# Adaptive-norm attention and feed-forward on one core: mixed adapter tiles moved into the down products, SyncE's queue re-ordered, style product issued a tile earlier, projections in the order Q, K, V

## What is computed

```python
W = weights[condition]                                # one 32x32 matrix per batch, of 16
h = einsum('bct,bcd->bdt', x, W)                      # "style" product
q, k, v = split(clip(einsum('bsd,ed->bse', h, w_qkv), -8, 8), 3)
q, k = layer_norm(q) * w + b, layer_norm(k) * w + b
p = softmax(q k^T * scale + alibi, causal)            # 32 heads of 16, 32 positions
x = x + einsum('bsd,ed->bse', p v, w_out)
y = einsum('bsi,boi->bso', x, weight[adapter_ids])    # one 512x512 adapter per batch, of 8
h = relu(y @ up_w) ** 2
shared = h @ down_w
routed = ((y @ fc1) @ expert) * sum(top2(y @ gate)) @ fc2
x = x + layer_norm(shared + routed) * gamma + beta
```

## Time and profile before

| | us |
|---|---|
| median of 3 runs | 1117.49 |
| lowest and highest | 1116.0, 1117.51 |
| the profiled execution, its own time | 1122.09 |
| its span in the trace | 1120.3 |
| TensorE busy within the span | 1063.7 (95%) |
| VectorE, ScalarE, GpSimd busy | 623.6, 572.7, 567.8 |

### The profile page before, as it was taken

One profiled execution on the slowest core, in us unless ns is written; L12 is line 12 of the kernel. 1 busy time (PEld: TensorE's weight loads), 2 busy tenths in 40 slices (PEclk: granted clock), 3 DMA queues, 4 the chain that ended last, 5 costly groups with the idle time before them and its releaser, 6 DMA issues.

```text
span 1120.3 us, 29460 instructions
## 1 busy us (share of the span) xinstructions
PE 1063.7 (95%) x12012; PEld 841.9 (75%) x12012; DVE 623.6 (56%) x1050; ACT 572.7 (51%) x955; POOL 567.8 (51%) x490
## 2 busy tenths in 40 slices
PE   5999999999999999999989995999999999999994
PEld 3878778888878887878777774675868777787883
DVE  4577767767675767676764333333544434454432
ACT  3576777777767778777774214224060514233220
POOL 5666877777776777776654222222242323233331
PEclk9999999999999999999999997999999999999997
DMA  6125454555545556556468835293616252130101
GB/s 254 62 79 174 170 185 168 178 189 173 192 149 178 177 190 202 182 169 171 153 242 305 316 102 152 67 215 105 168 64 202 65 192 64 64 85 29 47 29 37
DMA packets 99988, 166.59 MB, mean 149 GB/s; under 512 B 45648, under 2 KB 46416, under 8 KB 96016
## 3 DMA queue, kind: packets, MB, share of 16 engines
q1 hardware_dynamic: 90304, 140.97, 39.1%
q0 software_dynamic: 6064, 17.05, 5.2%
q10 hardware_dynamic: 3488, 6.70, 1.7%
HBM read 98.09 MB, written 40.89 MB: 124 GB/s over the span
## 4 chain that ended last, share of the span: by engine, by line
PE 82%; issue 4%; POOL 4%; DMA 3%; DVE 3%; ACT 2%; SPq 2%; ACTq 0%; POOLq 0%; DVEq 0%
PE banks L726 20%; PE pair L961 15%; PE banks L937 14%; PE banks L954 7%; PE banks L775 7%; PE banks L841 6%; PE pair L743 2%; PE banks L857 2%; PE pair L803 2%; POOL w_lo L1807 1%; PE banks L907 1%; PE banks L711 1%; DMA yT_lo<-y_part_low 1%; SPq L497 1%; POOL probs L1801 1%
## 5 line engine op out<-in xcount | busy, mean ns | idle before, releaser
L1807 POOL TENSOR_TENSOR w_lo<-w2t,w_hi 128x2048 fp32r<-128x2048 f32 x26 | 119.5, 4595 | 75.1 <-ACT w_hi L1129 75.1
L726 PE MATMUL banks<-wqkv_hi,h_hi 128*128 128x512 f32 x384 | 153.2, 399 | 3.2 <-DVE wqkv_lo L1604 0.5
L1872 POOL TENSOR_TENSOR u_lo<-act,u_hi 128x512 fp32r<-128x512 f32 x64 | 82.4, 1289 | 139.7 <-ACT u_hi L1342 139.7
L726 PE MATMUL banks<-wqkv_hi,h_lo 128*128 128x512 f32 x384 | 149.7, 390 | 0.0
L726 PE MATMUL banks<-wqkv_lo,h_hi 128*128 128x512 f32 x384 | 149.7, 390 | 0.0
L1896 POOL TENSOR_TENSOR frstd<-fve,cst 128x1 f32<-128x1 f32 x32 | 31.9, 997 | 186.4 <-DVE fve L1740 186.4
L1438 ACT ACTIVATE total<-banks,weight 128x512 f32<-128x512 f32 x32 | 22.0, 687 | 187.2 <-PE banks L954 187.2
L937 PE MATMUL banks<-yT_hi,up_hi 128*128 128x512 f32 x256 | 102.3, 400 | 11.9 <-ACT act L1338 11.9
L1733 DVE TENSOR_TENSOR total<-total,pair 128x512 f32<-128x512 f32 x32 | 22.0, 688 | 152.2 <-PE pair L961 152.2
L937 PE MATMUL banks<-yT_hi,up_lo 128*128 128x512 f32 x256 | 100.6, 393 | 0.0
L937 PE MATMUL banks<-yT_lo,up_hi 128*128 128x512 f32 x256 | 100.4, 392 | 0.0
(11 more groups left out here) (182 smaller groups left out, 2636.8 us busy)
## 6 DMA issues: line engine op xcount, KB each, us to landing
w2t<-in_w SPq DMA_DIRECT2D x26, 1024.0 KB
w<-in_w SPq DMA_DIRECT2D x24, 768.0 KB, 7.1
vx<-v_hl SPq DMA_DIRECT2D x128, 68.0 KB, 2.6
x1g<-x_rows SPq DMA_DIRECT2D x32, 256.0 KB, 2.8
kx<-k_hl SPq DMA_DIRECT2D x124, 64.0 KB
x_rows<-x1t SPq DMA_DIRECT2D x31, 256.0 KB, 2.3
y_rows<-ys SPq DMA_DIRECT2D x26, 256.0 KB, 3.3
w<-in_w SPq DMA_DIRECT2D x24, 256.0 KB, 2.8
```

Of the source, the lines that this page charges most:

```text
L726: m = e.matmul(into, a[:, c, :], b[:, n, c, :], start=(c == 0 and k == 0), stop=(c == KC - 1 and k == 2))
L1807: e.tensor_tensor(w2_lo[:, :, :], w2t[:, :, :], w2_hi[:, :, :].bitcast(F32), ALU.subtract).then_inc(d_wlo, 1)
L1872: e.tensor_tensor(u_lo[n % FC][:, :], act[n % 2][:, :], u_hi[n % FC][:, :].bitcast(F32), ALU.subtract) \
```

## The change

- late(m) is gone: the mixed tiles of all six groups are done among the down products (turn_mixed ahead of them; adapt_first after down(m, 0) and adapt_last after down(m, 1), in group 0 after down(0, 1) and down(0, 2)). Before, group 0 had them one tile later.
- SyncE's order is one for all: load_x1(4m+2), load_last(m); in group 0 then load_x1(3) and load_y(2) ahead of store_mixed(0); store_mixed(m), load_mixed(m+1), then load_x1(4m+3), load_y(m+2), and load_first(m+1) at the end.
- In attention, from tile 7 on, style is issued one iteration earlier and as its last product: style(i+2) after values(i-3) instead of style(i+1) after the projections. It now waits for add_x(i-4) of the same iteration (`upto(e, "x1", t - 6)` with t = i+2) and for slot_out of tile i-6. high_h and low_h of tile i+1 go to the start of the iteration on ScalarE and VectorE, GpSimd makes the style matrix one tile further ahead.
- The projections go in the order Q, K, V in all iterations; VectorE takes v after q and k. low_planes moves behind q's clip and statistics.
- In the drain, VectorE's last low_planes, low_o(T-4) and add_x(T-5), and ScalarE's high_o(T-4) come earlier.

```diff
--- before.py
+++ after.py
@@ -341,10 +341,6 @@
 
         return m < MIXED
 
-    def late(m):
-
-        return m < 2
-
     def upto(e, name, i):
 
         if i >= 0:
@@ -670,21 +666,22 @@
                     upto(e, "r", T - 1)
                     load_back(1, 0, 0, KC)
                     load_back(1, 1, 0, KC)
-                if late(m):
-                    load_x1(GROUP * m + 2)
+                load_x1(GROUP * m + 2)
                 if mixed_in(m):
                     load_last(m)
-                    if late(m):
-                        load_x1(GROUP * m + 3)
+                if m == 0:
+                    load_x1(3)
+                    load_y(2)
+                if mixed_in(m):
                     store_mixed(m)
-                    if mixed_in(m + 1):
-                        load_mixed(m + 1)
-                        load_first(m + 1)
-                if not late(m):
-                    load_x1(GROUP * m + 2)
+                if mixed_in(m + 1):
+                    load_mixed(m + 1)
+                if m:
                     load_x1(GROUP * m + 3)
-                if m + 2 < GROUPS:
+                if m and m + 2 < GROUPS:
                     load_y(m + 2)
+                if mixed_in(m + 1):
+                    load_first(m + 1)
 
             last_rows = [e.value_load(tile_rows[SEQ * b:SEQ * b + 1, TILES - 1:TILES], min_val=0, max_val=TOKENS - SEQ)
                          for b in range(BPT)]
@@ -702,7 +699,11 @@
                 upto(e, "x1", t - 6)
                 upto(e, "hlo", t - 1)
                 if style_tiled(t):
-                    upto(e, "cv", t - 1)
+                    upto(e, "cv", t - 2)
+                    if t == LAG + 1:
+                        upto(e, "klo", t - 3)
+                    else:
+                        e.wait_ge(d_mc, t - 1 - LAG)
                 for c in range(KC):
                     if style_tiled(t):
                         for k in range(2):
@@ -832,7 +833,7 @@
                     upto(e, "cq", s + LAG)
                     e.wait_ge(d_mc, s)
                 else:
-                    upto(e, "hlo", s + LAG + 1)
+                    upto(e, "cv", s + LAG)
                 pairs = [(xgT_hi, w2_lo, c) for c in range(KC)]
                 pairs += [(xgT_hi, w2_hi, c) for c in range(KC)] + [(xgT_lo, w2_hi, c) for c in range(KC)]
                 for k, (a, b, c) in enumerate(pairs):
@@ -928,7 +929,7 @@
                     e.wait_ge(m_up[1], 32)
                 if n >= 2:
                     e.wait_ge(S["relu"], n - 1)
-                if f == 1 and m and late(m - 1):
+                if f == 1 and m and mixed_in(m - 1):
                     e.wait_ge(d_mc, UNIFORM + m)
                 cols = slice(P * (f % KC), P * (f % KC) + P)
                 for c in range(KC):
@@ -947,8 +948,6 @@
                     e.wait_ge(m_down, 48)
                 if n >= 2:
                     e.wait_ge(S["tot"], n - 1)
-                if t == 1 and mixed_in(m) and not late(m):
-                    e.wait_ge(d_mc, UNIFORM + m + 1)
                 for c in range(KC):
                     for k, (a, b) in enumerate(((yT_hi, route_hi), (yT_hi, route_lo), (yT_lo, route_hi))):
                         i = e.matmul((B6, B7)[n % 2], a[m % 2][:, c, toks], b[:, c, :],
@@ -997,6 +996,8 @@
                 upto(e, "klo", i - 2)
                 if i > LAG:
                     e.wait_ge(d_mc, i - LAG)
+                if style_tiled(i + 1) and i + 1 < T:
+                    upto(e, "hlo", i + 1)
                 project(i, 2, B5, "pv")
 
             def turn_q(t):
@@ -1011,18 +1012,14 @@
             for i in range(T - 1):
                 if 0 < i < SHORT:
                     style(i + 1)
-                if i >= LAG:
-                    project_v(i)
                 project_q(i)
                 if i in (2, 3):
                     make_route(i - 1)
                 project_k(i)
                 if i == 0:
                     style(1)
-                if i < LAG:
-                    project_v(i)
+                project_v(i)
                 if i >= LAG:
-                    style(i + 1)
                     turn_slot(i - LAG, banks47)
                 if i >= 4:
                     turn_values(i - 4)
@@ -1041,6 +1038,8 @@
                     make_route(3)
                 if i >= 3:
                     values(i - 3)
+                if LAG - 1 <= i < T - 2:
+                    style(i + 2)
 
             project_q(T - 1)
             project_k(T - 1)
@@ -1085,18 +1084,9 @@
                     up(m, f)
                     if m == 0 and f == EARLY:
                         turn_gates(0)
-                    if mixed_in(m) and not late(m):
-                        if f == 3:
-                            e.wait_ge(S["route"], GROUP * m - 1)
-                            turn_mixed(m, B6)
-                        if f == 4:
-                            e.wait_ge(S["route"], GROUP * m)
-                            adapt_first(m, B7)
-                        if f == FC - 1:
-                            adapt_last(m, B7)
                 if ahead and m:
                     gate_products(m + 1)
-                if late(m):
+                if mixed_in(m):
                     e.wait_ge(S["relu"], FC * m + FC - 1)
                     turn_mixed(m, B2)
                 for t in range(GROUP):
@@ -1105,9 +1095,9 @@
                         gate_products(1)
                     if ahead and t == (0 if m else 2):
                         turn_gates(m + 1)
-                    if late(m) and t == (0 if m else 2):
+                    if mixed_in(m) and t == (0 if m else 1):
                         adapt_first(m, B3)
-                    if late(m) and t == (1 if m else 3):
+                    if mixed_in(m) and t == (1 if m else 2):
                         adapt_last(m, B3)
 
         @block.scalar
@@ -1293,7 +1283,7 @@
                                  scale=rstd[t % 2][:, n:n + 1]).then_inc(A[("qn", "kn")[n]], 1)
 
             for i in range(T - 1):
-                if i < SHORT:
+                if i < SHORT or i >= LAG:
                     high_h(i + 1)
                 if i == 0:
                     high_weights(3)
@@ -1314,7 +1304,6 @@
                 if i >= 1:
                     normalize(i - 1)
                 if i >= LAG:
-                    high_h(i + 1)
                     slot_in(i - LAG, banks47)
                 if i >= 4:
                     high_o(i - 4)
@@ -1366,9 +1355,9 @@
             scale_q(T - 2)
             high_q(T - 2)
             soft_exp(T - 3)
+            high_o(T - 4)
             scale_k(T - 1)
             high_k(T - 1, k_last)
-            high_o(T - 4)
             high_probs(T - 3)
             slot_out(LAST, B2)
             scale_q(T - 1)
@@ -1409,8 +1398,6 @@
                 ahead = m + 1 < GROUPS
                 for f in range(first_up(m), FC):
                     n = FC * m + f
-                    if mixed_in(m) and not late(m) and f == 4:
-                        mixed_turned(m, B6)
                     relu(n)
                     if ahead:
                         for c in turns(m, f):
@@ -1425,10 +1412,8 @@
                     high_u(n)
                 if ahead and m:
                     gates_out(m + 1)
-                if late(m):
+                if mixed_in(m):
                     mixed_turned(m, B2)
-                elif mixed_in(m):
-                    mixed_out(m, B7)
                 for t in range(GROUP):
                     n = GROUP * m + t
                     e.wait_ge(S["rp"], n + 1)
@@ -1639,24 +1624,22 @@
                 if i >= 4:
                     divide(i - 4)
                 if i >= LAG:
-                    take_v(i)
-                if i >= T - 8:
-                    low_planes(i - T + 8)
+                    low_h(i + 1)
                 take_q(i)
                 if i < SHORT:
                     low_h(i + 1)
                 stats_of(i, 0, qn, "cq")
+                if i >= T - 8:
+                    low_planes(i - T + 8)
                 if 0 <= i - 5 < CHUNKS:
                     low_chunk(i - 5)
                 take_k(i)
                 stats_of(i, 1, kn, "ck")
                 aggregate(i)
-                if i < LAG:
-                    take_v(i)
+                take_v(i)
                 if i == 0:
                     low_weights(3)
                 if i >= LAG:
-                    low_h(i + 1)
                     low_slot(i - LAG, banks47)
                 if i >= 4:
                     low_o(i - 4)
@@ -1683,6 +1666,7 @@
             divide(T - 5)
             take_q(T - 1)
             stats_of(T - 1, 0, qn, "cq")
+            low_planes(EARLY_GROUPS * KC - 1)
             take_k(T - 1)
             stats_of(T - 1, 1, kn, "ck")
             aggregate(T - 1)
@@ -1690,13 +1674,12 @@
             low_slot(LAST, B7)
             low_o(T - 5)
             low_k(T - 2, k_hl)
-            low_planes(EARLY_GROUPS * KC - 1)
             bias_max(T - 3)
```

(8 more changed lines are left out.)

## The result

| | us |
|---|---|
| before, median of 4 runs beside it | 1117.08 (1116.0 to 1117.51) |
| changed, median of 4 runs | 1154.37 (1151.76 to 1156.47) |
| ratio | 1.0334, 95% interval 1.0309 to 1.036: slower |
| profiled execution of the changed kernel | 1151.76, span 1150.0 |

The forecast was 1094.8 us. The feed-forward did nearly what was forecast, the attention did not: the span is 29.7 us longer, the feed-forward behind group 0 19.8 us shorter (714.37 to 1150.0 are 435.6 us; 664.89 to 1120.3 were 455.4), and all before it 49.5 us longer.

The account below looks back on a forecast made before the run. TensorE, busy 1063.7 of 1120.3 us, was taken as the bound. Feed-forward 21.68, drain 1.0 and steady attention 0 made 22.7 us off the median 1117.49: 1094.8 us, own range 1091 to 1098, with bounds and two rivals 1088.5 to 1101.

Parts of the forecast that it names:

- Feed-forward: Groups 1 to 5 lose their waits for transposes and cost 61.33 us each: a gain of 21.68 us.
- the wait for the last quarter of w4: Feed-forward: load_last behind load_x1 might make TensorE wait 0 to 0.5 us in each of five groups.
- Drain: End of attention: low_planes early lets kx be issued sooner; gain 1.0 us, bounds 0 and 3.7 us.
- the wait for kx: Drain: TensorE's 1.00 us wait for the kx DMAs, expected to go as kx is issued 3 us sooner.
- Steady attention: Attention iterations with style behind values: taken as 0, range -5 to +5 us over 25 iterations.
- VectorE and ScalarE get slack in every iteration: Attention: the argument for the rival in which attention gains 3 to 6 us more.
- My slower rival: Attention: add_x 1.5 us late for style on TensorE in all 25 iterations, +27.5 us, 1122; chance 0.03.
- the rule on instruction lines: TensorE: a line holds 16 KB or 256 instructions, only two lines; taken to give the sum no sign.
- Attention does not gain: Rival judged: attention gains 3 to 6 us more by fewer stalls at scores or a clean drain, 1090; chance 0.15.
- The front end does not pay a second 0.2 us: Rival judged: in attention TensorE's front end comes 0.2 us late a second time, +5 us, 1100; chance 0.12.
- the feed-forward gives only part: Rival: w4's last quarters or transposes late in each group, 1102 to 1108; chance 0.06.
- Low_planes against low_w2: Rival: in attention the two exclude each other, k's clip slips 4.6 us, +17 us, 1112; chance 0.03.

Follow-up runs that it names:

- e8: Kernel before with the feed-forward part of the change alone: 1100.73 us, ratio 0.9849 to the kernel before.
- e11: Kernel before with the feed-forward part alone, measured again: 1101.58 us, ratio 0.9854 to the kernel before.
- e1: Kernel before with the feed-forward and drain parts, attention in its old order: 1101.25 us, ratio 0.9864 to the kernel before.
- e12: Kernel before with the feed-forward and drain parts, measured again: 1102.45 us, ratio 0.9864 to the kernel before.
- e5: Changed kernel with GpSimd waiting for style's signal before it issues its two gathers: 1125.02 us, ratio 1.0086 to the kernel before.
- e9: Changed kernel with GpSimd's style product waiting for ScalarE's h_hi signal, not TensorE's style signal; gathers unmoved: 1122.32 us, ratio 1.0057 to the kernel before.
- e6: Changed kernel with style between the Q and K projections, high_h behind high_w2, low_h behind q's statistics: 1130.0 us, ratio 1.0113 to the kernel before.
- e10: Changed kernel with style between the Q and K projections, high_h ahead of high_w2, low_h ahead of q's statistics: 1103.71 us, ratio 0.9896 to the kernel before.
- e3: Changed kernel with high_h moved behind high_w2 and low_h behind q's statistics, style still behind values: 1150.55 us, ratio 1.0304 to the kernel before.
- e2: Changed kernel with GpSimd's two gathers moved behind low_probs in each steady iteration: 1135.88 us, ratio 1.0175 to the kernel before.
- e4: Changed kernel with style's semaphore raised by the Q projection's first matmul instead of style's last: 1153.22 us, ratio 1.0345 to the kernel before.

## Why the prediction was wrong

**Feed-forward: right in mechanism, 2 us off in the trace and 5 to 7 against the runs.** No idle time ahead of relu or the turned tile, load_y(2) in 10.34 us (10.4 to 11 expected), groups 1 to 5 at 61.58 to 61.80 instead of 61.33 us. The rest is the wait for the last quarter of w4 that I had bounded at 0 to 0.5 us in each of five groups and put at nothing in the sum; it is 1.9 us over 5, longest 0.5:

```profile
PE banks L858 <- DMA w<-in_w: 1.9, 5, 0.5
```

So 19.8 us in the trace. The runs give 15 to 17 (e8, e11): I took the whole sum off the median, but the profiled execution of before was 4.6 us above its median and that of e8 1.0 above its own, so some 3.6 us of what was saved were the profiled execution's. That is worked out from the times alone; no trace of a faster execution of the kernel before shows where it saves them.

**Drain: 1.0 us forecast, nothing in the medians.** The traces show 0.9 and 2.1 us less (e1 against e8, e12 against e11), the medians no gain. A wait at values for p_lo (1.2 us in e1) took the place of that for o_lo, as forecast; the wait for kx stayed (1.1 us in e1), which the forecast had taken off.

**Steady attention: the step that failed.** "I take 0 and keep 0 to +0.2 us x 25 iterations" was +49.5 us. I had costed style's new place on TensorE, with its wait for add_x, and not what the move did to ScalarE's queue: "VectorE and ScalarE get slack in every iteration" is the sentence that was wrong. High_h went to the head of ScalarE's iteration, ahead of the 3.9 us that lead to w_hi and so of the whole chain of w_lo, p_lo and exp. That alone put 25 iterations at the mercy of one signal. It was late by up to 2.9 us for a reason that no row of before shows, and cost 28 to 31 us (e5: ratio 1.0086, e9: 1.0057, against 1.0334). My slower rival had a wait in each of 25 iterations, as it came, but on the wrong engine and for the wrong thing, so that its "slower" came true by another mechanism.

The second part is 20 to 26 us: e9 against e12 is 1.0057 to 0.9864 (22 us by the ratios, 20 by the medians), e5 against e8 1.0086 to 0.9849 (26 and 24). I had met the rule on instruction lines, said that values and style (256 instructions in 1.9 us) speak against the change, and then let it cancel against the shorter stretch ahead of scores. It does not cancel. Of before, three iterations in 25 wait, 4.2 us in all; of the changed kernel ten have such a wait, and two of them a second, 22.7 us in all, and the clock behind the longer ones comes on top. That the rows of values and style and of turns and scores are now both 256 instructions long, where one was 320 and the other 192, was to be read from the code. The length of a row alone does not say whether it waits: the row of 320 had three waits before, and the row of turns and scores is still 256 long in e6 and e10, where the waits at its end fall to 7 and 4 us. Shown is that style right behind values brings these waits, and that they go when it is taken from there; why, beyond that they are instruction fetches, is open.

**Rivals.** Attention does not gain. The front end does not pay a second 0.2 us: most of e5's iterations without a nameless wait take 17.8 to 18.1 us, as before. That the feed-forward gives only part by late quarters of w4 is so for 1.9 us; that e8 and e11 (1100.7 and 1101.6) come near this rival's 1102 is mostly the 4.6 us by which the profiled execution lay above the median. Low_planes against low_w2: none of the eight low_planes meets it, all take 0.68 or 0.69 us in the changed kernel. The last one took 2.27 us before, beside p_lo; moved away from it, it takes 0.68.

## What to carry to other kernels

Before moving an instruction to the head of an in-order queue, write down what stands behind it and how often that chain goes round; at the head of ScalarE's queue a signal up to 2.9 us late cost some 1.2 us in each iteration. Moving the instruction back is no cure by itself: in e3 and e6 V's projection waited for its result instead. Where a kernel has stretches of small matmuls, count the instructions of a row and of a loop on TensorE: waits without a releaser that end just behind a 16 KB instruction packet, come back with a fixed period in iterations, and move when instructions are added far ahead of them, are instruction fetches. Here a full-array product between two rows took most of them away (e6, e10). And try the parts of a change by themselves: the feed-forward part alone is 1.5% faster than before, the whole 3.3% slower.

## What the runs showed of the hardware that was not expected

- A semaphore raised by TensorE while GpSimd issues two indirect DMAs (1.08 and 0.95 us) was recorded, and seen by ScalarE, 2.1 to 2.9 us late if GpSimd's program waits on that semaphore too, and 0.03 to 0.18 us late in 22 iterations of 25 if it does not (e9), or if the gathers are issued at another time (e2, e5: at most 0.05 us). It does not depend on which matmul raises it (e4). In the changed kernel all 22 late signals came 0.47 to 0.81 us behind the end of the second gather. ScalarE's signal of h_hi, for which GpSimd waits in e9, was not late among the gathers (24 times, within 0.01 us), and neither was TensorE's of the Q projection, for which GpSimd never waits (e5, 23 times, within 0.015 us). Why is open; only this one semaphore was taken away from GpSimd, and the first steady product of e3 and of e10 is not late though it ends among the gathers.
- TensorE's waits for instructions in the iterations of the kernels before and after ended 1.25 to 1.52 us behind the end of a 16 KB packet, had a period of nine iterations of 655 instructions, and moved by one iteration for 129 more instructions ahead.
